# Macaron block on one core: expert units of two batches, layer 1's parts straight from PSUM, layer 2's ReLU, cast and subtraction as 1024-column instructions

## The chip, the core and the metric

The kernel runs on one core of one Trainium2 chip. The metric is the device time in microseconds of one execution. Every number below is in microseconds (us) unless it says ns. The engines are TensorE (PE in the profile, PEld its weight loads), VectorE (DVE), ScalarE (ACT), GpSimd (POOL) and SyncE (SP, which here issues all DMAs).

## The reference

```
x = L0_attn_x                                  # 8 batches x 512 tokens x 128 features, float32
x = x + 0.5 * ffn(layernorm(x))
x = x + attention(layernorm(x))                # 16 heads of 64, one shared K and V head
x = x + 0.5 * ffn(layernorm(x))

def ffn(x):                                    # E = 8 experts, top 2, all layers 128 -> 128
    probs = softmax(x @ gate_w + gate_b, axis=tokens)
    vals, idx = top_k(probs, 2)
    h = relu(x @ w1[e] + b1[e])                # for every expert and every token
    h = relu(h @ w2[e] + b2[e])
    y = relu(h @ w3[e] + b3[e])
    v[e] = sum over batches and tokens of y * w_tok[b, s, e]
    return ind[b, s, e] @ v[e]                 # ind is 1 for the two chosen experts
```

Each of the two FFNs so computes three layers for 8 batches x 8 experts x 512 tokens.

## The kernel before, in words

All activations of an FFN lie transposed (128 features on the partitions, tokens along the free axis). A float32 product is made of three matmuls in a faster rounded type (fp32r): each operand is split into a high part (its rounded value) and a low part (what is left), and high x high, high x low and low x high are summed in PSUM (`product`, lines 509 to 513).

The experts' stage of each FFN (`experts`, one function per engine) works through 64 units m, a unit being one batch b and one expert e (m = 8b + e), 512 columns wide. A unit goes through:

- PE layer 1 (`layer1`, 3 matmuls), into one bank of the pair `psS`;
- ACT ReLU with bias into SBUF tile `t1` (named `xn` in the profile), line 826;
- DVE cast to the high part `h1h`, line 1031, and subtraction to the low part `h1l`, line 1033;
- PE layer 2 into the pair `psP`;
- ACT ReLU with bias into `t2` (named `t`), line 832, and ACT cast to `h2h`, line 836;
- POOL subtraction to `h2l`, line 464 (`R<-t,R` in the profile);
- PE layer 3 into the pair `psO`;
- DVE `scalar_tensor_tensor` (lines 1170 to 1172), which applies the third ReLU (as a maximum with the negated bias), multiplies by the tokens' gate weights `wbs` (part of `P_wb`) and accumulates along the row into `vacc`.

Every one of these buffers exists twice (index e % 2), so that a stage of unit m can run beside the next stage of unit m - 1. PE's order in a loop body (lines 616 to 623) is layer 1 of m + 4, layer 2 of m + 2, layer 3 of m. Each engine works its queue in order; they are tied by semaphores. SP brings the gate weights of one batch for all experts from DRAM (`wd`) as one 2048 KB broadcast, two batches ahead (`weights_out`, lines 338 to 359).

Before the experts' stage stands the gate: `gate_steps` (line 289) is one list of stages that every engine walks in the same order: normalise and transpose the batches ("turn"), logits, softmax in two groups of four batches ("bias", "exp", "probs"), the choice of the two experts ("choose", on DVE, `choose`, lines 1072 to 1097) and turning the chosen weights ("picks"). The first units' layers stand inside this list, so that the engines start on them while the second group is still being chosen. The transposed logits, picks and sums use the same eight PSUM banks as the experts. When the last accumulation is done, `update` (DVE line 1194 onwards) forms v and PE applies it to x.

Of the kernel before, what the change touches and what calls it, by code (L numbers as in the profile page):

```python
# [11 lines left out]
P = 128  # L12
# [15 lines left out]
def macaron_kernel(nc, x, Wq, bq, Wk, bk, Wv, bv, Wo, bo, gate_w, gate_b, w1, b1, w2, b2, w3, b3, out):  # L28
# [13 lines left out]
    NQ = B * QUADS  # L42
    SCALE = float(DK) ** -0.5
    assert D == P and E == 8 and DK == 64 and TPB == 4 and HPQ == 4

    with ExitStack() as ctx:
# [23 lines left out]
        bcol = sb("bcol", [P, ROWS])  # L70
        nb3 = sb("nb3", [P, E])
# [31 lines left out]
        vacc = sb("vacc", [P, E, B])  # L103
# [20 lines left out]
        MR = sb("MR", [P, 2, PAIRS, S], F32R)  # L124
# [15 lines left out]
        PT = picksT.rearrange("p u b t -> p (u b t)").rearrange("p (n s) -> p n s", s=S)  # L140
        xh = R[:, 0:E, :]
# [6 lines left out]
        h1h, h1l, h2h, h2l = (R[:, 2 * E + 2 * k:2 * E + 2 * k + 2, :] for k in range(4))  # L148
# [22 lines left out]
        s_nb3 = sem("negated_b3")  # L171
# [5 lines left out]
        def ffn_sems(f):  # L177
            names = ("xn_done", "xn_transposed", "xnT_ready", "logits_done", "gate_chain", "logits_biased",
                     "gate_exp", "probs_ready", "probs_transposed", "picked", "picks_transposed", "indT_ready",
                     "wT_ready", "wsum_done", "wd_written", "wb_loaded", "l1_done", "l2_done", "l3_done",  # L180
                     "relu1_done", "relu2_done", "l3_bank_free", "h1_high", "h1_ready", "h2_high", "h2_ready",
                     "x_low", "VB_zeroed", "v_chain", "v_ready", "v_transposed",
                     "VB_ready", "update_done", "x_updated")
            return {n: sem(f"f{f}_{n}") for n in names}

        F = [ffn_sems(0), ffn_sems(1)]
        s_wbf = [sem(f"wb_first_loaded{k}") for k in range(E // 2)]
# [100 lines left out]

        def gate_steps(f):

            part = [("stats", b) for b in range(TPB)]
            if f == 0:
# [4 lines left out]
                         ("layer1", 0), ("layer1", 1), ("choose", 0), ("picks", 0), ("probs", 1), ("split", 0), ("split", 1),  # L300
                         ("layer2", 0), ("layer1", 2), ("layer2", 1), ("layer1", 3), ("choose", 1), ("picks", 1)])
# [5 lines left out]
                     ("split", 0), ("exp", 1), ("layer1", 1), ("probs", 1), ("split", 1), ("layer2", 0), ("layer1", 2),  # L307
                     ("layer2", 1), ("layer1", 3), ("choose", 1), ("picks", 1)])
# [4 lines left out]
        def _(sp):  # L313
# [23 lines left out]

            def weights_out(f):

                s = F[f]  # L340
                for g in range(GROUPS):
# [5 lines left out]
                    if g == 0:  # L347
                        for k in range(E // 2):
                            sp.dma_start(wbs[0][:, 2 * k:2 * k + 2, :], wd[2 * k:2 * k + 2, 0, :, :]
                                         .rearrange("e j p -> e (j p)").partition_broadcast(P)).then_inc(s_wbf[k], 16)  # L350
                sp.wait_ge(s["wsum_done"], 1)
                sp.dma_start(wbs[1], wd[:, 1, :, :].rearrange("e j p -> e (j p)").partition_broadcast(P)
                             ).then_inc(s["wb_loaded"], 16)
                with sp.Fori(1, B // 2) as c:
                    for slot in range(2):

                        sp.wait_ge(s["l3_bank_free"], 2 + E * (2 * c + slot - 1) + 1)
                        sp.dma_start(wbs[slot], wd[:, bass.ds(2 * c + slot, 1), :, :].rearrange("e o j p -> e (o j p)")
                                     .partition_broadcast(P)).then_inc(s["wb_loaded"], 16)
# [49 lines left out]
        def _(pool):  # L409
# [49 lines left out]
            def experts(f):  # L459
                s = F[f]  # L460

                def split2(e, m):
                    pool.wait_ge(s["h2_high"], m + 1)
                    pool.tensor_tensor(h2l[:, e % 2, :], t2[:, e % 2, :], h2h[:, e % 2, :].bitcast(F32), ALU.subtract  # L464
                                       ).then_inc(s["h2_ready"], 1)

                def body(b):
                    for e in range(E):
                        split2(e, E * b + e)

                with pool.Fori(0, B) as b:
                    body(b)
                pool.wait_ge(s["h2_ready"], B * E)
                pool.memset(VB, 0.0).then_inc(s["VB_zeroed"], 1)
# [29 lines left out]
        def _(pe):  # L504
# [4 lines left out]
            def product(out, layer, e, high, low):  # L509

                pe.matmul(out, whi[:, layer, e, :], high, start=True, stop=False)  # L511
                pe.matmul(out, whi[:, layer, e, :], low, start=False, stop=False)  # L512
                return pe.matmul(out, wlo[:, layer, e, :], high, start=False, stop=True)  # L513


            def layer1(s, e, m, b):
                wait(pe, s["relu1_done"], m - 1)
                product(psS[e % 2][:, :], 0, e, xh[:, at(b), :].rearrange("p o s -> p (o s)"),
                        xl[:, at(b), :].rearrange("p o s -> p (o s)")).then_inc(s["l1_done"], 1)

            def layer2(s, e, m):
                pe.wait_ge(s["h1_ready"], m + 1)
                wait(pe, s["relu2_done"], m - 1)
                product(psP[e % 2][:, :], 1, e, h1h[:, e % 2, :], h1l[:, e % 2, :]).then_inc(s["l2_done"], 1)

            def layer3(s, e, m):
                pe.wait_ge(s["h2_ready"], m + 1)
                pe.wait_ge(s["l3_bank_free"], m + 1)
                product(psO[e % 2][:, :], 2, e, h2h[:, e % 2, :], h2l[:, e % 2, :]).then_inc(s["l3_done"], 1)

            def gate(f):
# [18 lines left out]
                for stage, arg in gate_steps(f):  # L550
# [19 lines left out]
                    elif stage == "picks":  # L570

                        pe.wait_ge(s["picked"], arg + 1)
                        if arg == 1:
                            pe.wait_ge(s["relu2_done"], 2)
                        elif f == 0:
                            pe.wait_ge(s_bc, 1)
# [6 lines left out]
                    elif stage == "layer1":  # L583
                        if arg == 0:
                            pe.wait_ge(s["x_low"], 1)
                            if f == 0:
                                pe.wait_ge(s_wl, 1)
                        if arg < 2:
                            pe.wait_ge(s["xnT_ready"], B - 1 + arg)
                        layer1(s, arg, arg, 0)  # L590
                    elif stage == "layer2":
                        if f == 0:
                            pe.wait_ge(s_wl, 2)
                        if arg == 0:
                            pe.wait_ge(s["wT_ready"], 1)
                        layer2(s, arg, arg)
# [11 lines left out]
            def experts(f):  # L608
# [7 lines left out]
                def body(b, has_next):  # L616
                    for e in range(E):
                        m = E * b + e
                        if e + 4 < E or has_next:
                            layer1(s, (e + 4) % E, m + 4, b if e + 4 < E else b + 1)  # L620
                        if e + 2 < E or has_next:
                            layer2(s, (e + 2) % E, m + 2)
                        layer3(s, e, m)

                body(0, True)
                with pe.Fori(1, B - 1) as b:
                    body(b, True)
                body(B - 1, False)
# [193 lines left out]
        def _(act):  # L822
            def relu1(s, e, m):
                act.wait_ge(s["l1_done"], m + 1)
                wait(act, s["h1_ready"], m - 1)
                act.activation(t1[:, e % 2, :], psS[e % 2][:, :], ACT.Relu, bias=bcol[:, R_B1 + e:R_B1 + e + 1]  # L826
                               ).then_inc(s["relu1_done"], 1)

            def relu2(s, e, m):
                act.wait_ge(s["l2_done"], m + 1)  # L830
                wait(act, s["h2_ready"], m - 1)
                act.activation(t2[:, e % 2, :], psP[e % 2][:, :], ACT.Relu, bias=bcol[:, R_B2 + e:R_B2 + e + 1]  # L832
                               ).then_inc(s["relu2_done"], 1)
# [11 lines left out]
            def gate(f):  # L845
                s = F[f]
                for stage, arg in gate_steps(f):
# [7 lines left out]
                    elif stage == "picks":  # L855
                        if f == 0:
                            act.wait_ge(s_wl, 2)
                        else:
# [26 lines left out]
            def experts(f):  # L885
                s = F[f]
                def body(b, has_next):
                    for e in range(E):
                        m = E * b + e
                        if e + 4 < E or has_next:  # L890
                            relu1(s, (e + 4) % E, m + 4)
                        if e + 2 < E or has_next:
                            relu2(s, (e + 2) % E, m + 2)

                body(0, True)
                with act.Fori(1, B - 1) as b:
                    body(b, True)
                body(B - 1, False)

# [86 lines left out]
        def _(dve):  # L986
# [41 lines left out]
            def split1(s, e, m):  # L1028
# [323 lines left out]
```

## Time and profile before

| what | us |
|---|---|
| median of 3 runs | 1159.49 (1155.8 to 1160.2) |
| the profiled execution | 1155.8, its span 1154.0 |
| first gate and experts' stage | 0 to 209.8 of the span |
| attention | 209.8 to about 930 |
| second gate and experts' stage | about 930 to 1138.9 |
| last update and output | 1138.9 to 1154.0 |

The page of the profile gives busy time by engine, busy shares in 40 equal slices of the span (28.9 us each), and the costliest groups of instructions by source line. The other views used are the table of stretches (busy time of each engine and its number of instructions between two times), the timeline (single instructions in order of time, with the idle time before them in brackets) and the view of one source line (shortest, median and longest duration).

### The profile page before, as it was taken

The page shows a single profiled execution, that of the slowest core. Times are in us where ns is not written, and L with a number is a line of the kernel's source. Part 1 is how long each engine was busy: PE and PEld are TensorE (multiplying, and loading weights), DVE is VectorE, ACT ScalarE, POOL GpSimd, SP SyncE. Part 2 cuts the span into 40 slices and gives each one's busy share as a digit, 9 for nine tenths or more (in the row PEclk, how much of TensorE's full clock was granted, in tenths as well). Part 3 has the DMA queues.
Part 4 walks back from the last instruction along what each step waited for, and adds up shares of the span by engine and source line. Part 5 has one row for each costly group of instructions (what it writes and reads, how often), then busy time and mean ns, then how long its engine had stood idle before and what let it go on. Part 6 is the DMA issues. An engine that isn't in the chain of part 4 may idle for free.

```text
span 1154.0 us, 16851 instructions
## 1 busy us (share of the span) xinstructions
PE 1063.4 (92%) x5671; PEld 609.8 (53%) x5671; DVE 886.0 (77%) x1333; ACT 670.9 (58%) x899; POOL 703.5 (61%) x367
## 2 busy tenths in 40 slices
PE   4599999659999999999999999999999976899996
PEld 1376666335645655645655655654654523666663
DVE  9989999786766866866866866866764576999996
ACT  3388888435654654654654654654654643788882
POOL 3465555527785785785685685686685861555552
PEclk8799999879999999999999999999999988899999
DMA  5165473000101001001001001001001012576672
GB/s 151 41 136 120 97 121 73 19 1 3 39 20 38 20 21 38 20 21 38 21 20 39 20 21 38 20 20 38 20 20 39 21 38 64 87 118 101 108 110 73
DMA packets 43850, 59.25 MB, mean 51 GB/s; under 512 B 9829, under 2 KB 23174, under 8 KB 43782
## 3 DMA queue, kind: packets, MB, share of 16 engines
q1 hardware_dynamic: 43782, 58.37, 24.2%
q8 instruction: 40, 0.66, 0.3%
q14 instruction: 28, 0.23, 0.1%
HBM read 55.20 MB, written 2.62 MB: 50 GB/s over the span
## 4 chain that ended last, share of the span: by engine, by line
PE 60%; issue 17%; POOL 16%; DVE 6%; ACT 1%; POOLq 0%; DMA 0%; SPq 0%
PE ring L737 19%; POOL R L464 13%; PE ring L690 5%; PE ring L708 5%; PE ring L710 5%; PE ring L712 5%; PE ring L714 5%; PE ring L747 4%; PE ring L723 3%; DVE xn L1054 2%; PE ring L672 2%; POOL sum_picksT L425 1%; PE ring L674 1%; PE ring L673 1%; PE ring L647 1%
## 5 line engine op out<-in xcount | busy, mean ns | idle before, releaser
L1238 DVE TENSOR_REDUCE mx<-ring 128x2 f32<-128x1024 f32 x256 | 298.6, 1225 | 88.1 <-PE ring L690 88.1
L425 POOL TENSOR_TENSOR sum_picksT<-sum_picksT,P_wb 128x1024 f32<-128x1024 f32 x128 | 323.9, 2531 | 18.6 <-POOL sum_picksT L425 0.4
L924 ACT ACTIVATE P_wb<-ring 128x1024 f32<-128x1024 f32 x256 | 262.3, 1028 | 64.8 <-PE ring L714 40.2
L464 POOL TENSOR_TENSOR R<-t,R 128x512 fp32r<-128x512 f32 x128 | 171.1, 1337 | 160.7 <-ACT R L836 160.6
L425 POOL TENSOR_TENSOR sum_picksT<-P_wb 128x1024 f32<-128x1024 f32 x64 | 153.8, 2403 | 172.7 <-ACT P_wb L924 172.7
L737 PE MATMUL ring<-P_wb,t 128*64 128x512 f32 x1024 | 226.8, 595 | 0.0
L511 PE MATMUL ring<-R,whi 128*128 128x512 f32 (+1 forms) x384 | 170.0, 443 | 18.5 <-DVE R L1033 9.6
L513 PE MATMUL ring<-R,wlo 128*128 128x512 f32 (+1 forms) x384 | 153.1, 399 | 0.0
L512 PE MATMUL ring<-R,whi 128*128 128x512 f32 (+1 forms) x384 | 152.8, 398 | 0.0
L936 ACT COPY OZ<-ring 128x512 f32<-128x512 f32 x64 | 37.0, 587 | 199.1 <-PE ring L737 156.5
L737 PEld LDWEIGHTS ring<-P_wb,t 128*64 128x64 f32 x1024 | 70.6, 137 | 132.8 <-issue 128.4
L1031 DVE CAST R<-xn 128x512 fp32r<-128x512 f32 x128 | 130.9, 1023 | 0.6 <-ACT xn L826 0.4
L511 PEld LDWEIGHTS ring<-R,whi 128*128 128x128 f32 x384 | 72.7, 189 | 92.8 <-issue 40.3
L690 PE MATMUL ring<-R 64*128 64x512 f32 x512 | 106.0, 411 | 6.2 <-DVE mx L1238 4.0
L832 ACT ACTIVATE t<-ring,bcol 128x512 f32<-128x512 f32 x128 | 88.3, 690 | 29.6 <-PE ring L513 27.2
L708 PE MATMUL ring<-R 64*128 64x512 f32 x512 | 102.8, 397 | 2.3 <-DMA MR<-mT 2.3
L710 PE MATMUL ring<-R 64*128 64x512 f32 x512 | 101.5, 392 | 0.0
L712 PE MATMUL ring<-R 64*128 64x512 f32 x512 | 101.1, 391 | 0.0
L1170 DVE SCALAR_TENSOR_TENSOR ring<-ring,nb,P_wb 128x512 f32<-128x512 f32 x128 | 96.1, 753 | 6.5 <-PE ring L513 3.9
L714 PE MATMUL ring<-MR,NEG 64*128 64x512 f32 x512 | 100.8, 390 | 0.0
L826 ACT ACTIVATE xn<-ring,bcol 128x512 f32<-128x512 f32 x128 | 88.2, 689 | 19.8 <-DVE R L1033 11.2
L1033 DVE TENSOR_TENSOR R<-xn,R 128x512 fp32r<-128x512 f32 x128 | 90.6, 708 | 4.4
(136 smaller groups left out, 1350.5 us busy)
## 6 DMA issues: line engine op xcount, KB each, us to landing
P_wb<-wd SPq DMA_DIRECT2D x14, 2048.0 KB, 15.5
rzb_indp<-rzd SPq DMA_DIRECT2D x64, 256.0 KB, 3.9
P_wb<-wd SPq DMA_DIRECT2D x8, 512.0 KB, 10.4
xs<-in_L_attn_x SPq DMA_DIRECT2D x8, 256.0 KB, 3.7
zrc<-SZ SPq DMA_DIRECT2D x128, 2.0 KB, 1.7
out<-xs SPq DMA_DIRECT2D x8, 256.0 KB, 2.5
sum_picksT<-in_L_ffn_w SPq DMA_DIRECT2D x2, 512.0 KB, 5.5
MR<-mT SPq DMA_DIRECT2D x64, 4.0 KB
```

What stands on the lines that cost most here:

```text
L425: pool.tensor_tensor(US[:, g % 2, c, :, :], first, PU[:, TPB * c + t, :, :], ALU.add).then_inc(s_ua, 1)
L464: pool.tensor_tensor(h2l[:, e % 2, :], t2[:, e % 2, :], h2h[:, e % 2, :].bitcast(F32), ALU.subtract).then_inc(s["h2_ready"], 1)
L511: pe.matmul(out, whi[:, layer, e, :], high, start=True, stop=False)
L513: return pe.matmul(out, wlo[:, layer, e, :], high, start=False, stop=True)
L690: mm = pe.matmul(banks[:, par, :], QH[rows, g % 2, c, P * j:P * (j + 1)], KH[rows, g // QUADS % 2, :], start=True, stop=True)
L708: pe.matmul(banks[:, par, :], KH[rows, kv, keys], QH[rows, g % 2, c, :], start=True, stop=False)
L710: pe.matmul(banks[:, par, :], KH[rows, kv, keys], QL[rows, g % 2, c, :], start=False, stop=False)
L712: pe.matmul(banks[:, par, :], KL[rows, kv, keys], QH[rows, g % 2, c, :], start=False, stop=False)
L714: mm = pe.matmul(banks[:, par, :], NEG[rows, :], MR[rows, g % 2, c, :], start=False, stop=True)
L737: mm = pe.matmul(ring[slot(("weigh", g))][DK * par:DK * (par + 1), c, :], Vn[:, g // QUADS % 2, t, :], PU[:, TPB * c + t, par, :], start=( ...
L924: act.activation(PU[:, u, :, :], ring[slot(("scores", g, u))][:, :, :], ACT.Exp, scale=SCALE).then_inc(s_exp, 1)
L1238: dve.tensor_reduce(mx[:, :, u], ring[slot(("max", g, u))][:, :, :], AX.X, ALU.max).then_inc(s_max, 1)
```

## The change

Two batches and one expert now make a unit u (32 per FFN, u = 8p + e for batches 2p and 2p + 1), 1024 columns wide, over a whole pair of banks. `expert_pair` gives layer 1 the pairs `ring0` and `ring1` in turn, layer 2 always `ring2`, layer 3 always `ring3`. `h1h` and `h1l` still exist twice; their second copy lies in `MR`. `t2`, `h2h` and `h2l` exist once, at double width.

ACT's ReLU of layer 1 and `t1` go. DVE makes both parts from PSUM as max(z, -b1), which is relu(z + b1) - b1; the missing b1 is put back by adding w2^T b1 to b2 once, from 8 one-column matmuls in the first gate. Layer 2's ReLU and cast (ACT), its subtraction (POOL) and the accumulation (DVE) are 1024-column instructions. `product` does the low-part matmuls last and waits for the low part only there. The gate weights come as one 512 KB broadcast per unit. The loops are unrolled.

```
 NU = B // 2 * E                                       # 32 units
 def product(pair, layer, e, high, low, low_ready=None):
     for k in range(2): pe.matmul(pair[:, k, :], whi[:, layer, e, :], high[:, k, :], ...)
     for k in range(2): pe.matmul(pair[:, k, :], wlo[:, layer, e, :], high[:, k, :], ...)
     for k in range(2):
         if low_ready is not None:
             pe.wait_ge(*low_ready(k))
         mm = pe.matmul(pair[:, k, :], whi[:, layer, e, :], low[:, k, :], ...)
     return mm
 def layer1(s, u):
     wait(pe, s["h1_ready"], u - 1)
     product(expert_pair(1, u), 0, e, xh[...], xl[...]).then_inc(s["l1_done"], 1)
 def layer2(s, u):
     pe.wait_ge(s["h1_high"], u + 1)
     wait(pe, s["relu2_done"], u)
     product(expert_pair(2, u), 1, u % E, h1h[u % 2], h1l[u % 2], lambda k: (s["h1_ready"], u + 1)).then_inc(s["l2_done"], 1)
 def layer3(s, u):
     pe.wait_ge(s["h2_high"], u + 1)
     wait(pe, s["l3_drained"], u)
     product(expert_pair(3, u), 2, u % E, h2h, h2l, lambda k: (s["h2_ready"], u + 1)).then_inc(s["l3_done"], 1)
 # PE, experts
     for u in range(NU):
         if u + 2 < NU: layer1(s, u + 2)
         if u + 1 < NU: layer2(s, u + 1)
         if u == 0:
             pe.wait_ge(s["indT_ready"], GROUPS)
             pe.wait_ge(s["wsum_done"], 1)
         layer3(s, u)
 # ACT
 def relu2(s, u):
     act.wait_ge(s["l2_done"], u + 1)
     wait(act, s["h2_ready"], u)
     act.activation(t2[:, :, :], expert_pair(2, u)[:, :, :], ACT.Relu, bias=bcol[:, e:e + 1]).then_inc(s["relu2_done"], 1)
     wait(act, s["l3_done"], u)
     act.wait_ge(s["relu2_done"], u + 1)
     act.copy(h2h, t2[:, :, :]).then_inc(s["h2_high"], 1)
 # POOL, experts
     for u in range(NU):
         pool.wait_ge(s["h2_high"], u + 1)
         pool.tensor_tensor(h2l, t2[:, :, :], h2h.bitcast(F32), ALU.subtract).then_inc(s["h2_ready"], 1)
 # DVE
 def split1(s, u):
     z = expert_pair(1, u)[:, :, :]
     dve.wait_ge(s["l1_done"], u + 1)
     wait(dve, s["l2_done"], u - 1)
     dve.tensor_scalar(h1h[u % 2], z, nb1[:, e:e + 1], None, ALU.max).then_inc(s["h1_high"], 1)
     dve.wait_ge(s["h1_high"], u + 1)
     dve.scalar_tensor_tensor(out=h1l[u % 2], in0=z, scalar=nb1[:, e:e + 1], in1=h1h[u % 2].bitcast(F32), op0=ALU.max,
                              op1=ALU.subtract).then_inc(s["h1_ready"], 1)
 # DVE, experts
     split1(s, 1)
     for u in range(NU):
         if u + 2 < NU: split1(s, u + 2)
         dve.wait_ge(s_wb[e], 16 * (B // 2 * f + p + 1))
         dve.wait_ge(s["l3_done"], u + 1)
         z = expert_pair(3, u)[:, :, :]
         dve.scalar_tensor_tensor(out=z, in0=z, scalar=nb3[:, e:e + 1], in1=PU[:, e, :, :], op0=ALU.max,
                                  op1=ALU.mult, accum_out=vacc[:, e, p:p + 1]).then_inc(s["l3_drained"], 1)
 # gate, f = 0 (second half of the list)
-    ("layer1", 0), ("layer1", 1), ("choose", 0), ("picks", 0), ("probs", 1), ("split", 0), ("split", 1),
-    ("layer2", 0), ("layer1", 2), ("layer2", 1), ("layer1", 3), ("choose", 1), ("picks", 1)
+    ("layer1", 0), ("choose", 0), ("picks", 0), ("probs", 1), ("split", 0),
+    ("layer2", 0), ("choose", 1), ("picks", 1), ("layer1", 1)
 # gate, f = 1 (end of the list)
-    ("turn", B - 1), ("layer1", 0), ("bias", 1), ("split", 0), ("exp", 1), ("layer1", 1), ("probs", 1), ("split", 1),
-    ("layer2", 0), ("layer1", 2), ("layer2", 1), ("layer1", 3), ("choose", 1), ("picks", 1)
+    ("turn", B - 1), ("layer1", 0), ("bias", 1), ("split", 0), ("exp", 1), ("probs", 1), ("layer2", 0), ("choose", 1),
+    ("picks", 1), ("layer1", 1)
 # gate, PE, stage layer1
-    pe.wait_ge(s["xnT_ready"], B - 1 + arg)
+    pe.wait_ge(s["xnT_ready"], B)                      # unit 0
+    pe.wait_ge(s["wT_ready"], GROUPS)                  # unit 1
 # gate, f = 0, stage weights 2: PE multiplies, DVE waits for it and adds
+    for e in range(E):
+        mm = pe.matmul(psP[1][:, e:e + 1], wraw[1][:, P * e:P * (e + 1)], bcol[:, R_B1 + e:R_B1 + e + 1], ...)
+    dve.wait_ge(s_b2m, 1)
+    dve.tensor_tensor(bcol[:, R_B2:R_B2 + E], bcol[:, R_B2:R_B2 + E], psP[1][:, 0:E], ALU.add).then_inc(s_b2, 1)
 # SP: load_wb(f, p, e), 512 KB; for p > 0 once the unit 8 before it is drained
+    sp.wait_ge(s["l3_drained"], E * (p - 1) + e + 1)
+    load_wb(f, p, e)
```

## Rows read from the trace of the kernel before

**Rows 1.** The page: busy us by engine (share of the span) x instructions
```profile
PE 1063.4 (92%) x5671; PEld 609.8 (53%) x5671; DVE 886.0 (77%) x1333; ACT 670.9 (58%) x899; POOL 703.5 (61%) x367
```

**Rows 2.** Groups of instructions, 84 to 205: busy us, mean ns | idle before, releaser
```profile
L1031 DVE CAST R<-xn 128x512 fp32r<-128x512 f32 x49 | 55.2, 1126 | 0.0
L1170 DVE SCALAR_TENSOR_TENSOR ring<-ring,nb,P_wb 128x512 f32<-128x512 f32 x51 | 38.3, 753 | 0.0
L1033 DVE TENSOR_TENSOR R<-xn,R 128x512 fp32r<-128x512 f32 x50 | 35.6, 712 | 1.7
```

**Rows 3.** Timeline, first experts' stage: start us, us, engine and line, [idle before]
```profile
197.00 1.29 POOL L464 TENSOR_TENSOR R<-t,R 128x512 fp32r<-128x512 f32 x1 [1.34 <-ACT R L836]
197.25 1.31 DVE L1031 CAST R<-xn 128x512 fp32r<-128x512 f32 x1
199.21 0.75 DVE L1170 SCALAR_TENSOR_TENSOR ring<-ring,nb,P_wb 128x512 f32<-128x512 f32 x1
199.21 1.28 POOL L464 TENSOR_TENSOR R<-t,R 128x512 fp32r<-128x512 f32 x1 [0.93 <-ACT R L836]
```

**Rows 4.** Stretches: us, busy (x instructions) of PE, PEld, DVE, ACT, POOL, clock
```profile
59.90:78.80 18.90, 18.90 (x83) 15.31 (x82) 17.07 (x32) 17.97 (x29) 14.29 (x9) 1.00 0.68 148
84.80:204.00 119.20, 113.88 (x435) 73.88 (x435) 117.52 (x196) 97.00 (x146) 63.20 (x49) 1.00 0.51 102
```

**Rows 5.** Views of single lines: shortest/median/longest ns, first to last start
```profile
L439 POOL TENSOR_TENSOR wqlo<-wos,wqhi x1: 2344/2344/2344, 208.5 to 208.5; 128x1024 fp32r<-128x1024 f32 x1
L425 POOL TENSOR_TENSOR sum_picksT<-sum_picksT,P_wb x128: 2350/2402/3170, 255.2 to 928.1; 128x1024 f32<-128x1024 f32 x128
L839 ACT CAST wqhi<-wos x1: 1040/1040/1040, 206.5 to 206.5; 128x1024 fp32r<-128x1024 f32 x1
L832 ACT ACTIVATE t<-ring,bcol x128: 677/690/694, 48.8 to 1134.2; 128x512 f32<-128x512 f32 x128
L1232 DVE SCALAR_TENSOR_TENSOR R<-ring,bcol,R x64: 729/750/754, 228.5 to 879.5; 128x512 fp32r<-128x512 f32 x64
```

**Rows 6.** Timeline, one unit from ACT to POOL, then the last unit's end
```profile
62.69 0.69 ACT L832 ACTIVATE t<-ring,bcol 128x512 f32<-128x512 f32 x1
63.46 0.62 ACT L836 CAST R<-t 128x512 fp32r<-128x512 f32 x1
64.16 1.44 POOL L464 TENSOR_TENSOR R<-t,R 128x512 fp32r<-128x512 f32 x1 [0.73 <-ACT R L836]
...
206.67 1.27 POOL L464 TENSOR_TENSOR R<-t,R 128x512 fp32r<-128x512 f32 x1 [1.34 <-ACT R L836]
207.99 0.50 PE L511 MATMUL ring<-R,whi 128*128 128x512 f32 x1 [1.36 <-POOL R L464]
208.99 0.76 DVE L1170 SCALAR_TENSOR_TENSOR ring<-ring,nb,P_wb 128x512 f32<-128x512 f32 x1 [1.49 <-PE ring L513]
209.84 0.22 DVE L1194 TENSOR_REDUCE vv<-vacc 128x8 f32<-128x64 f32 x1
```

**Rows 7.** Timeline, first gate: the second group's weights copied
```profile
55.37 0.59 ACT L861 COPY sum_picksT<-ring 128x512 f32<-128x512 f32 x1 [2.85 <-PE ring L580]
```

**Rows 8.** Timeline, second gate, and the end of the second stage
```profile
969.67 0.63 PE L512 MATMUL ring<-R,whi 128*128 128x512 f32 x1
970.10 0.63 PE L513 MATMUL ring<-R,wlo 128*128 128x512 f32 x1
...
970.65 1.92 PE L546 MATMUL ring<-sum_picksT,gws 128*32 128x512 f32 x2
972.61 0.75 DVE L1063 TENSOR_SCALAR P_wb<-ring,gbc 128x512 f32<-128x512 f32 x1 [4.33 <-PE ring L546]
976.71 0.48 DVE L1079 COPY P_wb<-ring 128x32 f32<-128x32 f32 x4
985.83 0.59 ACT L861 COPY sum_picksT<-ring 128x512 f32<-128x512 f32 x1 [4.90 <-PE ring L580]
1138.90 0.22 DVE L1194 TENSOR_REDUCE vv<-vacc 128x8 f32<-128x64 f32 x1
```

More of the change, by code:

```diff
@@ L146, in xnT @@
             return PT[:, b % PD, :] if f else OT[:, b, :]
-        h1h, h1l, h2h, h2l = (R[:, 2 * E + 2 * k:2 * E + 2 * k + 2, :] for k in range(4))
+        h1h, h1l = ([R[:, 2 * E + 2 * k:2 * E + 2 * k + 2, :], MR[:, k, :, :]] for k in range(2))
+        h2h, h2l = (R[:, 2 * E + 2 * k:2 * E + 2 * k + 2, :] for k in range(2, 4))
+        assert UNITS == E and PAIRS == 2
         def pair(name):
@@ L287, in misc_bank, with expert_pair @@
             return ring[slot(("misc", g))][:, k, :]
+        def expert_pair(layer, u):
+            return ring[u % 2 if layer == 1 else layer]
         def gate_steps(f):
@@ L460, in experts @@
                 s = F[f]
[L462 to L473, printed above, removed]
+                for u in range(NU):
+                    pool.wait_ge(s["h2_high"], u + 1)
+                    pool.tensor_tensor(h2l, t2[:, :, :], h2h.bitcast(F32), ALU.subtract).then_inc(s["h2_ready"], 1)
+                pool.wait_ge(s["h2_ready"], NU)
                 pool.memset(VB, 0.0).then_inc(s["VB_zeroed"], 1)
@@ L507, in _ @@
             pe.transpose(psP[0][:, 0:ROWS], brow[:, :], ident[0:ROWS, 0:ROWS]).then_inc(s_bt, 1)
[L509 to L529, printed above, removed]
+            def product(pair, layer, e, high, low, low_ready=None):
+                for k in range(2):
+                    pe.matmul(pair[:, k, :], whi[:, layer, e, :], high[:, k, :], start=True, stop=False)
+                for k in range(2):
+                    pe.matmul(pair[:, k, :], wlo[:, layer, e, :], high[:, k, :], start=False, stop=False)
+                for k in range(2):
+                    if low_ready is not None:
+                        pe.wait_ge(*low_ready(k))
+                    mm = pe.matmul(pair[:, k, :], whi[:, layer, e, :], low[:, k, :], start=False, stop=True)
+                return mm
@@ L573, in gate @@
                         if arg == 1:
[L574 removed]
+                            pe.wait_ge(s_b2, 1)
+                            if f == 1:
+                                pe.wait_ge(s_sz, NQ)
                         elif f == 0:
@@ L593, in gate @@
                             pe.wait_ge(s_wl, 2)
-                        if arg == 0:
-                            pe.wait_ge(s["wT_ready"], 1)
-                        layer2(s, arg, arg)
+                        pe.wait_ge(s["logits_biased"], GROUPS)
+                        layer2(s, arg)
+                    elif stage == "weights" and arg == 2:
+                        pe.wait_ge(s_wf, 64)
+                        pe.wait_ge(s_bc, 1)
+                        for e in range(E):
+                            mm = pe.matmul(psP[1][:, e:e + 1], wraw[1][:, P * e:P * (e + 1)], bcol[:, R_B1 + e:R_B1 + e + 1],
+                                           start=True, stop=True)
+                        mm.then_inc(s_b2m, 1)
                     elif stage == "sums":
@@ L614, in experts @@
                 pe.wait_ge(s["wT_ready"], GROUPS)
[L616 to L628, printed above, removed]
+                for u in range(NU):
+                    if u + 2 < NU:
+                        layer1(s, u + 2)
+                    if u + 1 < NU:
+                        layer2(s, u + 1)
+                    if u == 0:
+                        pe.wait_ge(s["indT_ready"], GROUPS)
+                        pe.wait_ge(s["wsum_done"], 1)
+                    layer3(s, u)
             def update(f):
@@ L886, in experts @@
                 s = F[f]
[L887 to L898, printed above, removed]
+                for u in range(1, NU):
+                    relu2(s, u)
             def x_turned(b, bank):
```

129 lines of the change are left out of this document (49 added, 80 removed).

## The prediction
> **What bounds the kernel now.** I read the page's busy line first, then the groups of instructions inside the first experts' stage, then single instructions there, then the seams between gate and stage, because the change touches only the two experts' stages and the gates before them. The busy line names PE (92% of the span) [rows 1], but that is an average over a long attention in which nothing changes. Inside the stage DVE is the limit: cast, subtraction and accumulation have almost no idle time before them [rows 2], and DVE is busy 117.5 of 119.2 us, PE 113.9 by records that overlap [rows 4]. The cast is the odd one: mean 1.13 us for 512 columns [rows 2]. The timeline shows why: a cast that starts at 197.25 beside a POOL subtraction of 197.00 to 198.29 lasts 1.31 us, to the end of POOL's and a little over; an accumulation beside POOL at 199.21 takes its usual 0.75 and POOL its usual 1.28 [rows 3]. So DVE loses time to POOL in the instruction that has only SBUF operands, not in the one that reads PSUM. The period is 119.2/49 = 2.43 us for a unit of 512 columns, 4.87 for two [rows 4]. PE alone would need less: in the first 18.9 us of the stage it ran 83 matmuls back to back, 0.228 each, 9 of them 2.05 [rows 4]. Missing records can make it 0.233.
>
> Whole stages, from the end of the copy of the second group's weights (call it W) to DVE's first instruction of the update: 55.96 to 209.84 is 153.9 in the first FFN [rows 6, 7], 986.42 to 1138.90 is 152.5 in the second [rows 8].
>
> **DVE's part of the change.** Per pair of batches DVE's records now add up to 2 x (1.13 + 0.71 + 0.75) = 5.18 [rows 2]; they overlap by some 0.3, which gives the 4.87. After it: three instructions with a PSUM source, 1024 columns. The nearest rows are 512 columns from PSUM, 0.75 [rows 5, 8]. Twice that is the upper bound, so at most 3 x 1.50 = 4.5; less the fixed part of three instructions it is nearer 4.0. No cast from SBUF is left for POOL to hold up. ACT's ReLU of layer 1 goes too (0.69 x 2 per pair). Both are gains only if nothing else closes the loop later than 4.0.
>
> The Trainium skill, "SBUF — State Buffer", § Who interferes with whom, says that a VectorE instruction with at most one SBUF input, outside the two-port modes, does not contend with GpSimd, and that otherwise one of the two blocks fully. The trace agrees, 0.75 and 1.28 side by side against the cast's 1.31 [rows 3]. By that rule POOL runs free in the new stage; were one SBUF input enough, POOL would be held up by two of DVE's three instructions, which is the slow rival below.
>
> **What is late next.** `t2`, `h2h` and `h2l` now exist once. ACT's ReLU of unit u waits for `h2_ready` of unit u - 1 (it overwrites `t2`), its cast waits for that ReLU, POOL waits for the cast, and only POOL's end releases the next ReLU. That is a closed ring with no overlap, where before two half-size copies let ACT run one unit ahead of POOL:
> - ReLU, 1024 columns: 0.69 for 512 [rows 5] plus what 512 more columns add on ACT, 1.04 (`wqhi` cast, 1024) - 0.62 (cast, 512) = 0.42 [rows 5, 6]: 1.11.
> - Cast, 1024 columns: the same form stands in the trace, 1.04 [rows 5].
> - Subtraction on POOL, 1024 columns, rounded output: 2.34 [rows 5]; the attention's 1024-column additions take 2.40 in the median, which I keep as upper bound [rows 5]. I take 2.36.
> - Three handovers. ReLU's end to cast 63.46 - 63.38 = 0.08, cast's end to POOL 64.16 - 64.08 = 0.08 [rows 6]. POOL to ACT is not in the trace; POOL to PE is 207.99 - 207.94 = 0.05 [rows 6]. I take 0.08, bounds 0.05 and 0.15.
> Sum: 1.11 + 1.04 + 2.36 + 0.24 = 4.75. Bounds: 4.65 with the shortest of each, 4.90 with the longest. So the steady period falls by only 0.1 of 4.87, 2 to 3%, although DVE's work falls by 0.9.
>
> Is anything later than this ring? PE: 18 x 0.228 to 0.233 = 4.1 to 4.2. After `h2_ready` of u it does the two low matmuls (about 0.8 to `l3_done`, from 207.99 to 208.99 less one matmul [rows 6]), layer 1 of u + 3 and layer 2 of u + 2 (12 x 0.23 = 2.8, done at 3.4), the high matmuls of layer 3, and waits from 4.3 to 4.75. Queued behind that wait is only the next round. ACT's cast also waits for `l3_done` of u - 1, which comes at 0.8 while the ReLU runs to 1.2: hidden, by 0.4. DVE's accumulation waits for `l3_done` and ends at 2.2; PE wants that bank at 3.4: hidden. The weights' broadcasts have a whole round of 8 units, some 38 us, to land; even a 2048 KB one of before was issued only two batches ahead. I cost them at nothing.
>
> **The ends of the stage.** Larger units fill and drain more slowly.
> - Start. Unit 1's layer 1 now waits for W, since its banks hold the weights. Before, four units' layer 1 and two whole ReLUs were done by W. From W: 6 matmuls (1.4 at full clock, 2.6 at half, 0.43 apart [rows 8]), then the matmul for the weights' sums, which DVE needs before it may start `split` 1 (W + 2.8 to 4.0); high part at + 1.3, low part at + 2.5 of that; layer 2's low matmuls and 0.7; ReLU, 1.1, and cast, 1.04, the cast after layer 3 of unit 0. POOL's unit 1 starts at W + 8.6 in the first FFN, W + 9.9 in the second, where the clock is low.
> - Middle: 30 periods of 4.75 = 142.5.
> - End: POOL 2.36, low matmuls to `l3_done` 0.8 (three took 1.05 [rows 6]), accumulation to the update's first instruction 1.4 (512 columns: 209.84 - 208.99 = 0.85 [rows 6]; bounds 0.85 and 1.6). 4.6.
> Sums: 155.7 against 153.9, + 1.8; 157.0 against 152.5, + 4.5.
>
> **The gates.** First FFN: DVE has to wait in "weights 2" for PE's eight one-column products, 1 to 3 us; POOL's weight subtractions hold DVE up in that stretch anyway, so that the choice ends up at the same place to within - 1 and + 2. I take + 0.2. Second FFN: layer 1 of unit 0 wants the last batch's transposed copy and so starts about 1.4 later than now, and it has 6 matmuls at half clock instead of 3 (0.43 each [rows 8], + 1.3); the last batch's logits stand behind it on PE, and DVE's bias waits for them (972.61 right behind 970.65 + 1.92 [rows 8]). That is + 2.6. From bias to the start of "choose" it is 976.71 - 972.61 = 4.1 now [rows 8]; then it is bias 1.4, split of 1024 columns 2.5, probs 0.6, and the transposes, which split 1 covered until now and which nothing covers then, 0.75: 5.2, + 1.1. Against that, POOL's 2.36 of unit 0 meets the chain of small DVE instructions once instead of twice 1.3, - 1 to + 0.3. I take + 3 in all, bounds + 1.5 and + 4.5.
>
> **Sum.** 1.8 + 4.5 + 0.2 + 3 = + 9.5 on the profiled execution's 1155.8: 1165.3. That execution is 3.7 below the median of the three runs, 1159.5, from which the same sum gives 1169. I predict 1167, between the two.
>
> **Rivals.**
> - Loop bound by PE, not by the ring (faster). If the ring did not close, because ACT or POOL work were shorter than their rows, the period would be PE's 4.2: 60 x 0.55 = 33 less, 1134. For it: PE's cadence is shown [rows 4]. Against it: every term of the ring is an instruction of the same width in the trace. 5 in 100.
> - A shorter ring (not slower). The records of ACT and POOL contain start-up that a waiting successor may partly overlap, and POOL's handover to ACT may be 0.05: period 4.60. That is 60 x 0.15 = 9 less: 1158, no change; it decides from a period of 4.63 on. For it: PE and DVE both leave room below 4.6. Against it: the handovers of 0.08 stand after the records' ends [rows 6]. 23 in 100.
> - POOL held up by DVE (slower still). DVE's instructions at twice the width meet every POOL instruction; if each meeting costs POOL 0.25, the period is 5.0: + 15, 1182. For it: DVE and POOL do hold each other up in this stage [rows 3]. Against it: not with PSUM sources [rows 3]. It decides from a POOL instruction of 2.5 on. 12 in 100.
> - My own case, ring of 4.75 and longer ends: 60 in 100, by itself 1160 to 1176.
>
> **Numbers.** A measurement here tells about 0.5%, 5.8 us, from no change: 1153.7 and 1165.3 are the limits. Faster: 5 from the first rival, 8 from the short ring with benign gates, 13 in 100. Same: 15 from the short ring, 12 from the low end of my case, 27. Slower: 48 from my case, 12 from the last: 60. The range, 1152 to 1179, leaves out the PE-bound case and the worse half of the last.
>
> **What would show it.** Right: in the stage POOL's subtractions 2.34 to 2.40 long and 4.75 apart, idle before each about 2.35 and released by ACT; ACT's ReLU released by POOL; PE idle once per unit before the first low matmul of layer 3, released by POOL; DVE's first part 1.2 to 1.5 and never stretched; W at about 56 and 989; the stages 156 and 157 long. Wrong: POOL 4.2 apart with PE never idle (first rival); POOL longer than 2.5 (last rival); idle DVE ended by a weights' DMA; ACT's cast released by PE.

## The result and the profile after

Before: median 1158.03 us (1155.8 to 1160.2, 4 runs). After: median 1176.22 us (1175.16 to 1176.96, 4 runs). The ratio is 1.0157, 95% interval 1.0132 to 1.0181: slower by 18 us. The forecast of 1167 had the direction and held the time in its range, but its sum was + 9.5 on the profiled execution; the profiled executions are 1155.8 and 1175.16, + 19.4. Half of the cost had been missed.

The page of the changed kernel: first busy us by engine (share of the span) x instructions, then two groups of instructions, and the weights' DMA with KB each and us to landing.

```profile
PE 1061.5 (90%) x5687; PEld 626.6 (53%) x5687; DVE 835.4 (71%) x1078; ACT 556.0 (47%) x643; POOL 686.2 (58%) x303
...
L468 POOL TENSOR_TENSOR R<-t,R 128x1024 fp32r<-128x1024 f32 x64 | 153.6, 2400 | 194.1 <-ACT R L837 194.1
...
L833 ACT ACTIVATE t<-ring,bcol 128x1024 f32<-128x1024 f32 x64 | 71.5, 1118 | 177.4 <-POOL R L468 154.7
...
P_wb<-wd SPq DMA_DIRECT2D x64, 512.0 KB, 3.6
```

Against [rows 1] DVE has 51 us less work, ACT 115, POOL 17 and PE 2, and the kernel got slower. No engine is near 100%: in this profile idle time, not busy time, is to be read. POOL's 194.1 us of idle time all end by ACT's cast, and most of ACT's by POOL: each of the two waits for the other. The weights land in 3.6 us, and nothing in the stage waits for them.

The table of stretches (us, busy of PE, PEld, DVE, ACT, POOL with instructions, granted clock, DMA share, GB/s): the first FFN stage's start, the same long stretch as in [rows 4], and the stage's end.

```profile
58.50:61.50 3.00, 2.94 (x7) 2.37 (x8) 0.00 (x0) 0.00 (x1) 0.00 (x0) 0.50 0.18 40
...
84.80:204.00 119.20, 109.74 (x443) 80.98 (x443) 95.62 (x99) 54.08 (x50) 58.45 (x25) 1.00 0.26 92
216.00:217.50 1.50, 1.22 (x2) 0.50 (x2) 0.00 (x0) 0.00 (x0) 1.44 (x3) 0.50 0.00 0
```

In the long stretch DVE fell from 117.5 to 95.6, and POOL has 25 subtractions where there were 49 of half the size. DVE is no longer the limit, and nothing took its place as a busy engine.

The waits inside the stage (84 to 205): who waited for whom, us in total, times, longest.

```profile
ACT t L833 <- POOL R L468: 64.7, 25, 2.9
POOL R L468 <- ACT R L837: 63.4, 26, 2.7
```

And the timeline: start, us, engine and line, [idle before <- releaser]. First the gate, then the stage's start, one steady unit, the last unit, and the second gate and stage.

```profile
34.68 4.95 POOL L443 TENSOR_TENSOR wlo<-sum_picksT,whi 128x1024 fp32r<-128x1024 f32 x2
...
35.38 0.16 DVE L1119 TENSOR_TENSOR bcol<-bcol,ring 128x8 f32<-128x8 f32 x1 [1.80 <-PE ring L604]
...
38.06 0.69 DVE L1054 TENSOR_REDUCE gst<-P_wb 128x1 f32<-128x512 f32 x1
...
47.80 0.59 ACT L863 COPY sum_picksT<-ring 128x512 f32<-128x512 f32 x1 [8.20 <-PE ring L583]
...
52.38 2.34 POOL L468 TENSOR_TENSOR R<-t,R 128x1024 fp32r<-128x1024 f32 x1 [10.37 <-ACT R L837]
52.44 2.43 DVE L1078 TENSOR_TENSOR P_wb<-P_wb,tm 128x128 f32<-128x128 f32 x1
...
55.83 1.12 PE L583 MATMUL ring<-ident,rzb_indp 128*128 128x128 f32 x4 [5.84 <-DVE P_wb L1087]
...
57.92 0.59 ACT L863 COPY sum_picksT<-ring 128x512 f32<-128x512 f32 x1 [5.61 <-PE ring L583]
...
62.37 0.42 DVE L1143 TENSOR_REDUCE wsum<-ring 128x8 f32<-128x256 f32 x1 [4.69 <-PE ring L615]
...
68.66 2.42 POOL L468 TENSOR_TENSOR R<-t,R 128x1024 fp32r<-128x1024 f32 x1 [13.94 <-ACT R L837]
...
119.78 1.12 ACT L833 ACTIVATE t<-ring,bcol 128x1024 f32<-128x1024 f32 x1 [2.58 <-POOL R L468]
...
120.99 1.05 ACT L837 CAST R<-t 128x1024 fp32r<-128x1024 f32 x1
...
121.91 1.28 DVE L1021 TENSOR_SCALAR R<-ring,nb 128x1024 fp32r<-128x1024 f32 x1
...
122.12 2.40 POOL L468 TENSOR_TENSOR R<-t,R 128x1024 fp32r<-128x1024 f32 x1 [2.43 <-ACT R L837]
...
124.57 0.72 PE L514 MATMUL ring<-R,whi 128*128 128x512 f32 x2 [0.36 <-POOL R L468]
124.61 1.12 ACT L833 ACTIVATE t<-ring,bcol 128x1024 f32<-128x1024 f32 x1 [2.57 <-POOL R L468]
...
213.85 2.37 POOL L468 TENSOR_TENSOR R<-t,R 128x1024 fp32r<-128x1024 f32 x1 [2.42 <-ACT R L837]
...
216.27 1.22 PE L514 MATMUL ring<-R,whi 128*128 128x512 f32 x2 [1.25 <-POOL R L468]
...
218.99 0.19 DVE L1171 TENSOR_REDUCE vv<-vacc 128x8 f32<-128x32 f32 x1
...
984.51 0.75 DVE L1053 TENSOR_SCALAR P_wb<-ring,gbc 128x512 f32<-128x512 f32 x1 [6.67 <-PE ring L547]
...
990.29 0.48 DVE L1069 COPY P_wb<-ring 128x32 f32<-128x32 f32 x4 [1.21 <-PE ring L569]
...
995.18 2.35 POOL L468 TENSOR_TENSOR R<-t,R 128x1024 fp32r<-128x1024 f32 x1 [13.70 <-ACT R L837]
...
997.37 0.59 ACT L863 COPY sum_picksT<-ring 128x512 f32<-128x512 f32 x1 [2.26 <-PE ring L583]
...
1007.71 2.40 POOL L468 TENSOR_TENSOR R<-t,R 128x1024 fp32r<-128x1024 f32 x1 [10.17 <-ACT R L837]
...
1152.57 2.36 POOL L468 TENSOR_TENSOR R<-t,R 128x1024 fp32r<-128x1024 f32 x1 [2.42 <-ACT R L837]
...
1157.70 0.19 DVE L1171 TENSOR_REDUCE vv<-vacc 128x8 f32<-128x32 f32 x1
```

The ring (the closed chain of ReLU, cast and subtraction through `t2`) can be read straight off: ReLU 119.78, cast 120.99, subtraction 122.12, next ReLU 124.61, which is 4.83 later. PE does the low matmuls at 124.57, also released by POOL. The copies at 57.92 and 997.37 answer to [rows 7] and [rows 8]; their ends are W, the moment from which the stage is counted, 58.51 and 997.96; 213.85 to 218.99 answers to the end in [rows 6]. The first stage, from W to DVE's first instruction of the update, is 160.5 long instead of 153.9, the second 159.7 instead of 152.5. DVE's parts take 1.28 beside POOL and are not stretched.

### The profile page after: what moved, and what is told of

It is laid out like the page before. It is cut to its first block, busy times and chain, and to the rows that moved or that the text cites. A ratio compares the mean times of both kernels' runs of the same rounds, so it can differ in the third digit from the quotient of the medians.

```text
span 1173.4 us, 15294 instructions
## 1 busy us (share of the span) xinstructions
PE 1061.5 (90%) x5687; PEld 626.6 (53%) x5687; DVE 835.4 (71%) x1078; ACT 556.0 (47%) x643; POOL 686.2 (58%) x303
## 4 chain that ended last, share of the span: by engine, by line
PE 61%; POOL 14%; ACT 12%; DVE 10%; issue 2%; ACTq 0%; DMA 0%; SPq 0%; POOLq 0%; DVEq 0%
PE ring L743 18%; POOL R L468 13%; ACT t L833 6%; ACT R L837 6%; PE ring L696 5%; PE ring L714 5%; PE ring L720 5%; PE ring L718 5%; PE ring L716 5%; PE ring L753 5%; PE ring L729 3%; DVE xn L1044 2%; PE ring L678 2%; POOL sum_picksT L429 1%; PE ring L679 1%
## 5 line engine op out<-in xcount | busy, mean ns | idle before, releaser
L468 POOL TENSOR_TENSOR R<-t,R 128x1024 fp32r<-128x1024 f32 x64 | 153.6, 2400 | 194.1 <-ACT R L837 194.1
L833 ACT ACTIVATE t<-ring,bcol 128x1024 f32<-128x1024 f32 x64 | 71.5, 1118 | 177.4 <-POOL R L468 154.7
L514 PE MATMUL ring<-R,whi 128*128 128x512 f32 x320 | 110.0, 426 | 25.1 <-POOL R L468 25.1
L1156 DVE SCALAR_TENSOR_TENSOR ring<-ring,nb,P_wb 128x1024 f32<-128x1024 f32 x64 | 82.7, 1292 | 66.1 <-PE ring L514 66.1
L508 PE MATMUL ring<-R,whi 128*128 128x512 f32 x320 | 103.9, 406 | 5.9 <-ACT R L837 3.2
L510 PE MATMUL ring<-R,wlo 128*128 128x512 f32 x320 | 102.7, 403 | 0.0
L514 PEld LDWEIGHTS ring<-R,whi 128*128 128x128 f32 x320 | 57.0, 194 | 61.6 <-POOL R L468 52.1
L1233 DVE TENSOR_TENSOR OT_xnT<-OZ,rzb_indp 128x1024 f32<-128x1024 f32 x32 | 73.9, 2310 | 7.1 <-DMA rzb_indp<-rzd 7.1
L508 PEld LDWEIGHTS ring<-R,whi 128*128 128x128 f32 x320 | 60.7, 192 | 21.7 <-ACT R L837 4.1
L696 PEld LDWEIGHTS ring<-R 64*128 64x128 f32 x512 | 49.0, 187 | 41.9 <-issue 23.9
```

Of the source, the lines that this page charges most:

```text
L468: pool.tensor_tensor(h2l, t2[:, :, :], h2h.bitcast(F32), ALU.subtract).then_inc(s["h2_ready"], 1)
L508: pe.matmul(pair[:, k, :], whi[:, layer, e, :], high[:, k, :], start=True, stop=False)
L514: mm = pe.matmul(pair[:, k, :], whi[:, layer, e, :], low[:, k, :], start=False, stop=True)
L696: mm = pe.matmul(banks[:, par, :], QH[rows, g % 2, c, P * j:P * (j + 1)], KH[rows, g // QUADS % 2, :], start=True, stop=True)
```

## The experiments

All but one start from the changed kernel; ratios are against the kernel before. The questions: is the closed ring really what the stage costs, and through which of the single buffers does it close (`t2`, `h2h`, `h2l`)? And what is each half of the change worth alone?

**`t2` twice.** The second copy takes the place of `t1`, which the change had freed.

```
+t2s = (t2[:, :, :], t1[:, :, :])
-wait(act, s["h2_ready"], u)          # ReLU
+wait(act, s["h2_ready"], u - 1)
 # ReLU, cast and subtraction use t2s[u % 2]
```

> The changed kernel with two copies of t2 (the buffer of the removed layer 1 ReLU serves as the second), so that the ReLU of unit u waits only for POOL's unit u - 2. Theory (the ring ReLU 1.12, cast 1.05, POOL 2.40, three handovers 0.26 = 4.83 closes through t2): that ring opens, and the next one, through the single h2h/h2l, takes over: cast 1.05 + POOL 2.40 + two low matmuls to l3_done 0.8 + two handovers 0.17 = 4.4. Period 4.4, 60 x 0.43 = 26 us less than the changed kernel's 1176: about 1150. Rival (single h2h and h2l hold the loop, or PE's order with the low part last): no change, 1172 to 1178.

Measured: 1148.14 (1147.15 to 1151.11), ratio 0.9902 (0.9884 to 0.992): 28 us below the changed kernel. The waits between 100 and 200 of this kernel:

```profile
POOL R L469 <- ACT R L838: 44.9, 23, 2.0
ACT t L834 <- PE ring L515: 21.0, 12, 1.8
...
ACT R L838 <- PE ring L515: 9.9, 23, 0.4
```

The ReLU waits for PE now, not for POOL. But each cast waits 0.4 for PE's end of layer 3, one step further round: a second ring stands behind the first. Its timeline:

```profile
123.66 2.40 POOL L469 TENSOR_TENSOR R<-xn,R 128x1024 fp32r<-128x1024 f32 x1 [1.94 <-ACT R L838]
...
126.11 0.74 PE L515 MATMUL ring<-R,whi 128*128 128x512 f32 x2
...
126.89 1.05 ACT L838 CAST R<-t 128x1024 fp32r<-128x1024 f32 x1 [0.44 <-PE ring L515]
...
128.02 2.40 POOL L469 TENSOR_TENSOR R<-t,R 128x1024 fp32r<-128x1024 f32 x1 [1.96 <-ACT R L838]
```

Subtraction 2.40, low matmuls 0.74, cast 1.05 and three handovers of 0.05, 0.04 and 0.08 make 4.36; the starts are 4.36 apart.

**`h2h` and `h2l` twice, `t2` once.** The second copies take tiles that hold attention weights only later.

```
-h2h, h2l = (R[...] for k in range(2, 4))
+h2h, h2l = ([w[:, :].rearrange("p (c s) -> p c s", c=2), R[...]] for k, w in enumerate((wqhi, wqlo)))
-wait(act, s["l3_done"], u)           # cast
+wait(act, s["l3_done"], u - 1)
```

> The changed kernel with two copies of h2h and h2l (the even units' in the tiles of the Wq parts, which nothing uses during an experts' stage), t2 still single. Theory (the ring through t2): period stays 4.83, time within 0.3% of 1176. Rival (h2h/h2l hold the loop): period falls to PE's 4.2, time to about 1140.

Beside these lines, ACT's cast that fills the tile `wqhi` for the attention now waits until the stage no longer uses it. Measured: 1175.66 (1174.1 to 1176.53), ratio 1.0145 (1.0127 to 1.0163), no different from the changed kernel. Its waits between 100 and 200 are still the pair of ACT and POOL:

```profile
ACT t L834 <- POOL wqlo L469: 28.5, 11, 2.6
...
ACT t L834 <- POOL R L469: 25.7, 10, 2.6
```

So the binding buffer is `t2`, as the prediction's ring has it. A second copy of a buffer that is not on the binding ring is worth nothing as long as that ring is closed; the next experiment shows what the same copies are worth once it is open.

**Both twice.**

> Both edits together: two copies of t2 and of h2h/h2l. Theory: no ring is left below PE's 18 matmuls of 0.233; period 4.2, 60 x 0.63 = 38 us less than 1176: about 1138, which beats the kernel before by 1.7%. If PSUM's single pairs for layers 2 and 3 close a ring of their own, 4.3 to 4.5 and 1145 to 1155. Rival (the wide instructions are too slow whatever the buffers): 1165 or more.

Its edit is the two above together. Measured: 1136.03 (1133.43 to 1139.17), ratio 0.9809 (0.9779 to 0.984): 40 us below the changed kernel and 12 below `t2` twice alone. Its timeline:

```profile
124.88 2.42 POOL L470 TENSOR_TENSOR R<-xn,R 128x1024 fp32r<-128x1024 f32 x1 [1.77 <-ACT R L839]
...
127.00 0.63 PE L512 MATMUL ring<-R,wlo 128*128 128x512 f32 x2
...
127.47 0.63 PE L516 MATMUL ring<-R,whi 128*128 128x512 f32 x2
...
129.07 2.43 POOL L470 TENSOR_TENSOR wqlo<-t,wqhi 128x1024 fp32r<-128x1024 f32 x1 [1.78 <-ACT wqhi L839]
```

Period 4.19, as expected, and PE's pairs of matmuls start 0.467 apart without a gap, 0.233 each: 18 of them make 4.20. POOL's instruction is no shorter than in the changed kernel (2.42 here, 2.40 there); only its idle time fell, from 2.43 to 1.77. This is the prediction's first rival, bound by PE, reached by opening both rings.

**Layer 1's parts from PSUM, alone.** The kernel before, 512 columns, every buffer still twice; ACT's first ReLU goes, DVE makes both parts from PSUM, b1 moves into b2.

```
-dve.tensor_copy(h1h[:, e % 2, :], t1[:, e % 2, :])
+dve.tensor_scalar(h1h[:, e % 2, :], z, nb1[:, e:e + 1], None, ALU.max)
-dve.tensor_tensor(h1l[:, e % 2, :], t1[:, e % 2, :], h1h[...].bitcast(F32), ALU.subtract)
+dve.scalar_tensor_tensor(out=h1l[:, e % 2, :], in0=z, scalar=nb1[:, e:e + 1], in1=h1h[...].bitcast(F32),
+                         op0=ALU.max, op1=ALU.subtract)
```

> The kernel before with only one part of the change: layer 1's parts made by DVE straight from PSUM, b1 moved into b2, no layer 1 ReLU on ACT; units of one batch and 512 columns, all buffers twice, loops and order as before. Theory: DVE's three instructions per unit take 0.75 + 0.75 + 0.81 less overlaps = 2.2 and POOL no longer stretches one of them, PE needs 2.1: period 2.15 to 2.25 instead of 2.40, 61 x 0.2 x 2 = 24 us less than 1158, plus about 2 for DVE's wait for the b1 products: about 1136. Rival (the parts from PSUM are themselves what makes the change slow, since layer 1's banks are held until both parts are made): 1158 or more, with PE waiting for DVE before layer 1.

Measured: 1134.27 (1132.83 to 1135.87), ratio 0.979 (0.9772 to 0.9807). Its timeline:

```profile
125.25 1.29 POOL L466 TENSOR_TENSOR R<-t,R 128x512 fp32r<-128x512 f32 x1 [0.89 <-ACT R L840]
...
126.07 0.75 DVE L1178 SCALAR_TENSOR_TENSOR ring<-ring,nb,P_wb 128x512 f32<-128x512 f32 x1
...
127.35 1.29 POOL L466 TENSOR_TENSOR R<-t,R 128x512 fp32r<-128x512 f32 x1 [0.81 <-ACT R L840]
```

A half unit every 2.10, PE's 9 x 0.233, while DVE's instructions keep to 0.75 beside POOL (all 128 that make the high part took 0.742 to 0.752), where the cast had 1.13 in the mean [rows 2]. So the first half of the change alone gains 25 us (2.1%; the kernel before ran at 1159.1 beside it). How much of that comes from the cast that POOL no longer stretches, and how much from the ReLU that is gone, was not separated. The second half, wide and single-buffered, with its gates in new order, costs 42 us on top of it. With all buffers twice the wide form comes to the same 1136 as the narrow one: with both loops at PE's bound the wider instructions gain nothing in the loop.

**The seams.** Three edits of the changed kernel: the matmul for the weights' sums goes ahead of unit 1's layer 1; DVE's wait for the b1 products moves from the weights stage to the first split; in the second gate the last group's bias comes before layer 1 of unit 0, and its split after exp and probs.

```
-("layer1", 0), ("bias", 1), ("split", 0), ("exp", 1), ("probs", 1), ("layer2", 0), ...
+("bias", 1), ("layer1", 0), ("exp", 1), ("probs", 1), ("split", 0), ("layer2", 0), ...
```

> The changed kernel, its experts' loop untouched, with three edits at the seams: the matmul for the weights' sums ahead of unit 1's layer 1, so that DVE need not wait for that layer before its split of unit 1; DVE's wait for the b1 products moved from the first gate's weights stage to just before its first split; in the second gate the last batch's logits ahead of unit 0's layer 1, and probs ahead of the split. Theory (what the steady ring does not explain of the +18 lies in the gates and in the start of each stage): about 1.3 less at each stage's start, 1 to 2 less in the first gate, 2 to 3 less in the second, 6 in all: 1170. The ring's period stays 4.83. Rival (the rest of the loss is spread over attention or is noise between executions): 1174 to 1178.

Measured: 1171.29 (1168.14 to 1172.47, 6 runs), ratio 1.0102 (1.0082 to 1.0122), 5 below the changed kernel. Rows of its timeline:

```profile
46.41 0.59 ACT L863 COPY sum_picksT<-ring 128x512 f32<-128x512 f32 x1 [9.97 <-PE ring L583]
...
56.53 0.59 ACT L863 COPY sum_picksT<-ring 128x512 f32<-128x512 f32 x1 [4.64 <-PE ring L583]
...
57.30 0.42 DVE L1144 TENSOR_REDUCE wsum<-ring 128x8 f32<-128x256 f32 x1 [1.01 <-PE ring L594]
...
65.89 2.43 POOL L468 TENSOR_TENSOR R<-t,R 128x1024 fp32r<-128x1024 f32 x1 [11.57 <-ACT R L837]
```

The first copy of the chosen weights comes at 46.41 instead of 47.80, the sums are read at W + 0.2 (57.30 - 57.12) instead of W + 3.9, and POOL's unit 1 starts at W + 8.8 instead of W + 10.15. Not shown as rows: the second gate is 1.0 shorter (below), and in the second stage POOL's unit 1 starts at W + 8.64 instead of W + 9.75, 1.1 less. The four gains, 1.4, 1.4, 1.0 and 1.1, add up to the 5 between the medians. The two profiled executions are only 2.8 apart, because the attention, whose code is the same, took 1.9 longer in this one.

**Both rings open and the seams.**

> Both buffers twice, with the same three edits at the seams. Theory: the two gains add, because the seams lie outside the loop: 1136 - 6 = 1130, the best of all. Rival (with the loop bound by PE, work taken from the start is only given back at PE): 1134 to 1138.

Its edits are those of "both twice" and "the seams" together. Measured: 1129.92 (1126.96 to 1132.28, 5 runs), ratio 0.9762 (0.9743 to 0.9781). It is the fastest of all, 29 below the kernel before (1159.0 beside it) and 46 below the changed one, as the sum of the two single gains (40 and 5) has it. It is also 4 below the narrow kernel with layer 1's parts alone (1134.27; the runs, 1127.0 to 1132.3 and 1132.8 to 1135.9, do not meet); whether the narrow kernel would gain as much from seams of its own was not tried.

## Why the prediction was right in kind and half in size

The forecast's and the measured differences, all between the two profiled executions:

| step | forecast | measured |
|---|---|---|
| ring's period, 60 of them | 4.75 | 4.840 and 4.829: + 5.1 in all |
| POOL's unit 1 after W, first stage | 8.6 | 68.66 - 58.51 = 10.15: + 1.55 |
| the same, second stage | 9.9 | 1007.71 - 997.96 = 9.75: - 0.15 |
| last subtraction to update | 4.6 twice | 5.14 and 5.13: + 1.1 |
| first gate | + 0.2 | 58.51 - 55.96 = + 2.55: + 2.35 |
| second gate | + 3 | + 2.0: - 1.0 |
| attention, last update and output | 0 | + 0.4, + 0.6: + 1.0 |
| sum missed | | 9.9 |

**The mechanism held.** The ring closes through `t2`, POOL's idle time is 2.43 (about 2.35 forecast) and ends by ACT, ReLU's by POOL, PE waits once per unit before the low matmuls, DVE is neither stretched nor late. Doubling `t2` opened the ring (28 us) and doubling the others did not. The slow rival (POOL held up by DVE) falls: POOL takes 2.40, under its limit of 2.5. The short ring (4.60) falls by the same rows. The PE-bound rival was right about what PE can do, 4.19, and wrong about this kernel. That the range held the time owes something to luck: my own case was to give 1160 to 1176, and the measured 1176.2 lies at its very end, by errors that mostly went one way. One sign contradicted the sum: by its terms W of the second stage was due at 986.4 + 1.8 + 0.2 + 3 = 991.4, not 989; it came at 998.0.

**The terms that failed: first the ring's length, then the first gate and the first stage's filling.** The ring's is the largest; with 4.83 in its place the sum would have been + 14.6 instead of + 9.5, so it is about half of the miss. Each piece of the ring was a little short: POOL 2.40 where I took 2.36, ReLU 1.12 for 1.11, cast 1.05 for 1.04, three handovers 0.09 + 0.08 + 0.09 = 0.26 for 0.24. Together 0.08, 1.7% of the ring and within its bounds of 4.65 to 4.90; but it is paid 60 times, 5 us. The row that I should have taken for POOL was the 2.40 of the attention [rows 5], which is measured with DVE at work beside it; the 2.34 was one instruction. In the gate with DVE held, the same instruction takes 2.34 again (52.38), in the stage 2.40, and the last one, with little DVE work beside it, 2.37 (213.85).

**Filling and draining at half clock.** In the first stage I took the six matmuls from W at full clock, because before the change PE had the full clock there. Now the granted clock is 0.50 from 58.5 to 61.5, and the sums' result is read at W + 3.86, the late end of what I gave. PE had less to do before W, since fewer layers run ahead in the gate: it was busy 2.0 of the 8 us before it (50.5 to 58.5), against 4.7 of 7.9 in the kernel before. That this is what let the clock fall was not tested. With the late end I would have had 9.9, as in the second stage, where that was taken and came out. The experiment on the seams gets 1.4 back by order alone; the granted clock from 56.6 to 59.0 is 0.50 there too. The drain is the same story in small: after a wait of 1.25 us PE's last two low matmuls run at clock 0.50 and take 1.22 instead of 0.72; in the second stage they take 1.22 as well. Before, the last three ran at full clock, and behind a longer wait, 1.36 ([rows 6], 207.99); in the changed kernel itself two matmuls at 213.82 stand behind a wait of 1.61 and still run at 1.00. So the last wait by itself does not explain it. What differs is the work before it: in the 4.7 us before these last matmuls PE was busy 1.9 now, 2.5 in the kernel before. No run varied that alone. With it the end is 5.1, not 4.6.

**First gate.** I let DVE's wait for the b1 products vanish behind POOL's weight subtractions. It is 1.80 long (35.38), and moving it brings the first copy forward by 1.4 (47.80 to 46.41): it was on the path. The other 1.1 lies between the first and the second copy, 8.99 before, 10.12 now, 10.12 in the seams' experiment as well. There POOL's 2.34 of unit 0 falls into the choice and holds a DVE instruction of 0.29 for 2.43, + 2.1; before, two of POOL's 1.3 held two such instructions, + 2.0, so this alone is no loss. Nearly all of the 1.1 lies behind the choice, where PE turns the chosen weights. Before, the row was this:

```profile
54.19 0.66 PE L580 MATMUL ring<-ident,rzb_indp 128*128 128x128 f32 x4 [3.04 <-DVE P_wb L1097]
```

From there to W it was 1.8 (54.19 to 55.96) at a granted clock of 1.00; now it is 2.7 (55.83 to 58.51) at 0.50. That is 0.9 more, the same half clock as in the filling. With `h2h` and `h2l` twice unit 0 came 1.3 later, at 53.7, behind the choice, and the stretch took 7.30, which is 2.8 less: 2.1 of it is the collision, the rest lies behind the choice, where the clock was 0.77 in the mean. So the place of one POOL instruction gives or takes 2 us. The same list in the kernel with `t2` twice ended at 61.23; these rows of its timeline say why.

```profile
34.91 4.70 POOL L444 TENSOR_TENSOR wlo<-sum_picksT,whi 128x1024 fp32r<-128x1024 f32 x2
...
35.83 6.35 DVE L1060 TENSOR_SCALAR P_wb<-P_wb,gst 128x512 f32<-128x512 f32 x1
...
39.57 2.33 POOL L444 TENSOR_TENSOR wlo<-t,whi 128x1024 fp32r<-128x1024 f32 x1
```

A 0.49 us instruction was held across three POOL subtractions in a row; in the changed kernel the same instruction, met by the same three, was let through after the first and took 1.72. Gates of the same code so differ by 5 us between kernels (55.9 to 61.2), and of the first gate's + 2.55 I call only the 1.4 of the b1 wait shown by an experiment.

**Second gate.** From the turn of the last batch, bias comes 2.3 later (forecast 2.6), bias to choice takes 5.8 instead of 4.1, + 1.7 (forecast 1.1), and the choice to W 7.7 instead of 9.7 (forecast - 1 to + 0.3): POOL's unit 0 starts at 995.18, after DVE's chain, and meets nothing. Inside the bounds, by errors of both signs. The new order gains 1.0 of it (turn to W 19.05 instead of 20.06): bias comes 2.4 sooner after the turn, but POOL's unit 0 then meets the choice again, and the choice to W takes 9.4 instead of 7.7.

Attention and the last update, + 1.0 together, had no term in the sum; why they differ stays open. Two executions of the same attention code differed by more, 1.9, between the changed kernel and the seams' experiment.

**What I didn't ask.** The sum compared the ring to the old period, 4.87, and found them close. But DVE's work was to fall from 5.18 to 4.0 per pair and PE needs 4.2, so the sum for the first half of the change alone would have shown 4.2. I had every number for that and did not price the halves apart.

## What to carry to other kernels

When a change makes instructions wider and pays for it with buffers that then exist once, add up the chain through each buffer that is written again (all its instructions and handovers, none overlapped) and compare it to the busiest engine before anything else; here a second copy of the buffer on the longest such ring gained 28 us, while copies elsewhere gained nothing until that ring was open, and 12 us then. A period is paid as often as the loop turns, so its terms deserve rows taken under the same company of engines, and the fill and drain of larger units should be priced at both clock levels: here the filling of the first stage and the last matmuls of both ran at a granted clock of 0.50, where the smaller units had run at 1.00. Price a change of two parts part by part: here one part alone gained 25 us and the other, added to it, lost 42.

## What the runs showed of the hardware

- A POOL subtraction of 1024 columns took 2.34 while DVE stood still and 2.40 while DVE worked with a PSUM source beside it (up to 2.43 with both rings open). DVE's own instructions of that kind kept their 1.28. If the difference comes from running side by side, which no run varied alone, that costs 2.5%, on POOL's side.
- DVE's element by element instructions with SBUF operands only were held by POOL's: a `tensor_tensor` of 0.29 took 2.43, a `tensor_scalar` of 0.49 took 6.35 across three POOL instructions in a row, but 1.72 in the changed kernel, where it was let through after the first. A `tensor_reduce` was not held: 0.69 (38.06) inside POOL's 34.68 to 39.63.
- In the drain the granted clock was at 0.50 for the last two matmuls, behind a wait of 1.25 us, in a stage that had run at 1.00; it was still 1.00 behind waits of 1.61 (the unit before) and 1.36 (the kernel before).
- A handover by semaphore took 0.04 to 0.09 us: POOL to PE 0.05, PE to ACT 0.04, ACT to ACT 0.09, ACT to POOL 0.08, POOL to ACT 0.09.
